# Time mixing moved from the weights to the data, and clamps and rounding moved to GpSimd, in an RWKV block with a gated FFN

## The reference

```python
xn = layernorm(x)
shifted = pad(xn, one token in front)[:, :-1]
k = (xn * mk + shifted * (1 - mk)) @ Wk          # v and r likewise, r through a sigmoid
# wkv: for each channel a recurrence over the 512 tokens, with a running maximum mx,
#   max_st = max(mx + td, k); num = e1s * num + e2s * v; den = e1s * den + e2s
s = (r * wkv) @ Wo
h = relu(xn @ w1[0] + b1[0])                     # expert 0 of the FFN alone has a weight
y = xn + h @ w2[0] + b2[0]
g = silu((y - mean(y)) * rsqrt(var(y) + 1e-5) * gamma + beta)
out = x + s * g
```

## Time and profile before

| | us |
|---|---|
| median of 3 runs | 128.43 (127.83 to 128.73) |
| the profiled execution | 127.27 |
| its span, first to last instruction | 125.4 |
| mean granted TensorE clock of it | 0.986 of full speed |

### The profile page before, as it was taken

How to read it: one execution, slowest core, us unless ns; L and a number is a source line. 1 busy time by engine, 2 the same in 40 slices (tenths; PEclk the granted TensorE clock), 3 DMA queues, 4 the chain that set the end, 5 groups by cost and what they waited for, 6 DMA issues and landing times.

```text
span 125.4 us, 1838 instructions
## 1 busy us (share of the span) xinstructions
PE 113.8 (91%) x448; PEld 77.4 (62%) x448; DVE 97.5 (78%) x206; ACT 105.9 (84%) x163; POOL 57.4 (46%) x87
## 2 busy tenths in 40 slices
...
GB/s 108 320 342 152 3 0 0 5 0 3 3 0 0 0 0 0 5 84 3 0 0 0 0 84 0 3 89 0 0 0 0 84 0 61 23 3 84 10 73 84
DMA packets 9433, 5.09 MB, mean 41 GB/s; under 512 B 464, under 2 KB 9168, under 8 KB 9424
## 3 DMA queue, kind: packets, MB, share of 16 engines
...
...
## 4 chain that ended last, share of the span: by engine, by line
PE 54%; DVE 2%; ACT 2%; issue 2%; ACTq 1%
PE ps_z L596 14%; PE ps_s L570 4%; PE ps_up L525 4%; PE ps_up L529 4%; PE ps_up L526 4%; PE ps_s L605 3%; PE ps_v L525 2%; PE ps_v L529 2%; PE ps_v L526 2%; PE ps_r L529 2%; PE ps_r L526 2%; PE ps_r L525 2%; PE ps_k L526 1%; PE ps_k L529 1%; PE ps_k L525 1%
## 5 line engine op out<-in xcount | busy, mean ns | idle before, releaser
L596 PE MATMUL ps_z<-hid,w_c 128*128 128x512 f32 x64 | 29.7, 594 | 0.0
L395 ACT ACTIVATE hid<-ps_up,vec 128x512 f32<-128x512 f32 x32 | 21.2, 682 | 2.5 <-PE ps_up L529 2.4
L596 PEld LDWEIGHTS ps_z<-hid,w_c 128*128 128x128 f32 x64 | 11.7, 190 | 10.1 <-issue 8.0
L323 POOL TENSOR_TENSOR dv<-v_sb 128x512 f32<-128x512 f32 x8 | 8.3, 1037 | 21.0 <-ACT v_sb L442 21.0
L315 POOL TENSOR_TENSOR sq_lo<-sq,sq_hi 128x512 fp32r<-128x512 f32 x8 | 11.0, 1371 | 12.6 <-ACT sq L403 12.0
L307 POOL TENSOR_SCALAR xn<-x_sb,neg_mean,rstd 128x128 f32<-128x128 f32 x28 | 16.7, 607 | 0.0
L525 PE MATMUL ps_up<-xT_hi,w_hi 128*128 128x512 f32 x32 | 16.3, 511 | 0.2
L739 DVE TENSOR_TENSOR_SCAN den<-e_keep,e_new 128x512 f32<-128x512 f32 x8 | 10.1, 1268 | 5.1 <-ACT e_new L428 4.7
L529 PE MATMUL ps_up<-xT_lo,w_hi 128*128 128x512 f32 x32 | 12.7, 398 | 0.0
L526 PE MATMUL ps_up<-xT_hi,w_lo 128*128 128x512 f32 x32 | 12.7, 397 | 0.0
L344 ACT ACT_TABLE_LOAD x8 | 10.3, 1283 | 2.4 <-issue 2.2
...
## 6 DMA issues: line engine op xcount, KB each, us to landing
...
vec<-vectors ACTq DMA_DIRECT2D x1, 6.0 KB, 3.2
```

Of the source, the lines that this page charges most:

```text
L395: act.activation(hid[b % 2][:, f, :], ps_up[f % 2][:, :], ACT.Relu, bias=vec[:, B1_COLUMN + f:B1_COLUMN + f + 1]).then_inc(done[f"hid{f}"], 1)
L596: ins = pe.matmul(ps_z[:, :], w2_c[:, f, :], hid[b % 2][:, f, :], start=False, stop=last)
```

## The change

- Token shift: the transposes now write into one of two banks `ps_z[b % 2]`, ACT copies it to an fp32 tile `xT` with one column of zeros in front (step `xT`), POOL makes `before_k`, `before_v`, `before_r` = shifted xT * (1 - m) (`Bk`, `Bv`, `Br`), DVE makes `mixed_k` and so on = `ps_z` * m + before (`ink`, `inv`, `inr`), and each projection is one fp32 matmul with the unchanged weights. The parts `w_now` and `w_before` are gone.
- `cx` is gone: the transposes leave their accumulation group open, and `z0` to `z3` add onto them.
- `xT_hi` is rounded from `xT` by POOL (by ACT for sequence 0), `w1_lo`, `gap_min` and `gap_max` are POOL's too, the last two with a second operation that changes nothing.
- One square, `sq` in fp32, and one fp32 matmul for `var`, now into the bank `ps_s`, which `s` and `back` share. `sq_hi` and `sq_lo` are gone.
- `th_r` writes back into `ps_r`, and `gated` reads it there.
- For sequence 7 the steps from `sq` to `res` and the store (`HALVED`) are issued in two halves of 256 tokens, in banks of their own.
- All four orders are new.

The diff, cut to its core:

```diff
     "pe": """
+        T:0 b2m up0:0 up3:0 k:0 up2:0 up1:0 z3:0 z2:0 z0:0 T:1 z1:0 v:0 up1:1 var:0 up0:1 k:1 up3:1 r:0
+        up2:1 T:2 z1:1 z0:1 z3:1 z2:1 up0:2 up1:2 var:1 v:1 up3:2 up2:2 k:2 T:3 r:1 z3:2 z1:2 z2:2 z0:2 k:3
+        up0:3 up1:3 var:2 up3:3 up2:3 s:0 v:2 z0:3 T:4 z1:3 z2:3 z3:3 back:0 up0:4 var:3 up1:4 r:2 k:4 s:1
+        up2:4 v:3 T:5 z0:4 up3:4 z2:4 r:3 z3:4 z1:4 k:5 var:4 up0:5 up1:5 v:4 back:1 up2:5 T:6 up3:5 s:2
...
     "act": """
+        ln_exp ve0 rs0 w1_hi neg_td xT:0 xT_hi:0 hid0:0 wo hid3:0 hid2:0 hid1:0 xT:1 e_keep:0 e_new:0 sq:0
+        v_sb:0 hid1:1 ln_den:0 ln_var:0 hid0:1 rstd2:0 silu_set th_g:0 th_a:0 xT:2 hid3:1 hid2:1 th_r:0
+        ln_exp e_keep:1 sq:1 hid0:2 e_new:1 hid1:2 ln_var:1 v_sb:1 rstd2:1 ln_den:1 hid2:2 hid3:2 xT:3
+        silu_set th_r:1 th_g:1 silu:0 th_a:1 sq:2 ln_exp e_keep:2 hid1:3 hid0:3 e_new:2 ln_var:2 hid3:3
...
     "dve": """
+        bnA:0 bnB:0 aggr1:0 norm1:0 bn:1 aggr1:1 one_minus cols xT_lo:0 w2_sum ink:0 bn:2 inr:0 aggr1:2
+        inv:0 mx:0 gap:0 bn:3 bn:4 aggr1:3 bn:5 xT_lo:1 den:0 ink:1 rel:0 inr:1 mx:1 zn:0 inv:1 aggr1:4
+        gap:1 dev:0 xT_lo:2 adev:0 ink:2 wkv:0 gated:0 inr:2 den:1 zn:1 rel:1 inv:2 mx:2 ink:3 gap:2 xT_lo:3
+        bn:6 inr:3 dev:1 aggr1:5 mx:3 gap:3 adev:1 wkv:1 inv:3 den:2 zn:2 bn:7 rel:2 aggr1:6 prod:0 den:3
+        xT_lo:4 res:0 ink:4 gated:1 dev:2 inv:4 adev:2 wkv:2 zn:3 inr:4 mx:4 rel:3 prod:1 gated:2 ink:5
...
     "pool": """
+        w1_lo neg_mean1:1 Bk:0 Br:0 Bv:0 w2_c rstd1:1 norm1:1 gap_min:0 gap_max:0 xT_hi:1 neg_mean1:2 Bk:1
+        Br:1 rstd1:2 Bv:1 norm1:2 dv:0 keep:0 xT_hi:2 Br:2 Bk:2 gap_max:1 neg_mean1:3 gap_min:1 rstd1:3 Bv:2
+        norm1:3 dv:1 neg_mean1:4 Bk:3 Br:3 xT_hi:3 keep:1 rstd1:4 gap_max:2 gap_min:2 neg_mean1:5 Bv:3
+        gap_max:3 gap_min:3 norm1:4 dv:2 neg_mean1:6 Bk:4 xT_hi:4 rstd1:5 keep:2 Br:4 Bv:4 norm1:5 rstd1:6
...
-        ps_x = bank("ps_x", T)
         ps_k = bank("ps_k", T)
         ps_v = bank("ps_v", T)
         ps_r = bank("ps_r", T)
         ps_up = [bank(f"ps_up{i}", T) for i in range(2)]
-        ps_z = bank("ps_z", T)
+        ps_z = [bank(f"ps_z{i}", T) for i in range(2)]
         ps_s = bank("ps_s", T)
-        ps_rows = ps_s[:, :].rearrange("p (j c) -> p j c", c=P)
+
+
+        def ps_var(half):
+            return {"": ps_s, "a": ps_up[0], "b": ps_up[1]}[half]
+
+        def ps_out(half):
+            return {"": ps_s, "a": ps_s, "b": ps_r}[half]
+
+        def ps_rows(half):
+            return {"": ps_s, "a": ps_k, "b": ps_v}[half][:, :].rearrange("p (j c) -> p j c", c=P)
...
+            def w1_low():
+                pool.wait_ge(prep["w1_hi"], 1)
+                pool.tensor_tensor(w1_parts[1][:, :], w1_in[:, :], w1_parts[0][:, :].bitcast(FP32),
+                                   ALU.subtract).then_inc(prep["w1_lo"], 1)
+
+            def high_part(b):
+                n = b % 2
+                after(pool, "xT", b)
+                for step in [f"up{f}" for f in range(NF)] + ["xT_lo"]:
+                    after(pool, step, b - 2)
+                pool.tensor_copy(xT_hi[n][:, :], xT[n][:, 1:]).then_inc(done["xT_hi"], 1)
+
+            def share_before(name):
+                which = "kvr".index(name)
+
+                def step(b):
+                    n = b % 2
+                    once(pool, b, "edges", EDGES)
+                    once(pool, b, "one_minus", 1)
+                    after(pool, "xT", b)
+                    after(pool, "in" + name, b - 2)
+                    pool.tensor_scalar(before[name][n][:, :], xT[n][:, 0:T], one_minus[:, which:which + 1], 0.0,
+                                       ALU.mult, ALU.add).then_inc(done["B" + name], 1)
+                return step
+
+            def lower(b):
+                n = b % 2
+                once(pool, b, "cols", 4)
+                after(pool, "gap", b)
+                after(pool, "e_new", b - 2)
+                pool.tensor_scalar(gap_min[n][:, :], gap[n][:, :], td[:, :], LOWEST, ALU.min,
+                                   ALU.max).then_inc(done["gap_min"], 1)
+
+            def upper(b):
+                n = b % 2
+                once(pool, b, "cols", 4)
+                after(pool, "gap", b)
+                after(pool, "e_keep", b - 2)
+                pool.tensor_scalar(gap_max[n][:, :], gap[n][:, :], td[:, :], HIGHEST, ALU.max,
+                                   ALU.min).then_inc(done["gap_max"], 1)
...
+                for step in ("Bk", "Bv", "Br", "xT_hi"):
                     after(act, step, b - 2)
-                act.activation(xT_hi[n][:, 1:], ps_x[:, :], ACT.Copy).then_inc(done["xT_hi"], 1)
+                act.activation(xT[n][:, 1:], ps_z[n][:, :], ACT.Copy).then_inc(done["xT"], 1)
...
+                act.activation(sq[b % 2][:, c], ps_z[b % 2][:, c], ACT.Square, bias=cb2[:, :]).then_inc(done["sq"], 1)
...
+                act.activation(ps_r[:, :], ps_r[:, :], ACT.Tanh, scale=0.5).then_inc(done["th_r"], 1)
...
             def transposes(b):
-                bank_x_free("T", b)
+                after(pe, "zn", b - 2)
                 if b > 0:
                     after_rows(pe, b)
                 for j in range(NT):
                     if b == 0:
                         pe.wait_ge(done["norm1"], j + 1)
-                    ins = pe.transpose(ps_x[:, j * P:(j + 1) * P], xn[b % 2][:, j, :], ident[:, :])
+
+                    ins = pe.matmul(ps_z[b % 2][:, j * P:(j + 1) * P], xn[b % 2][:, j, :], ident[:, :], start=j == 0,
+                                    stop=False, is_transpose=True, skip_group_check=True)
                 ins.then_inc(done["T"], 1)
...
+            def projection(name, dst, held):
                 which = "kvr".index(name)
-                now, before = ([part[:, :] for part in parts[which]] for parts in (w_now, w_before))
 
                 def step(b):
-                    n = b % 2
-                    once(pe, b, "w_hi_" + name, 2)
-                    once(pe, b, "w_lo_" + name, 2)
-                    once(pe, b, "edges", EDGES)
-                    after(pe, "xT_hi", b)
+                    if b == 0:
+                        pe.wait_ge(got["squares"], 16)
+                    after(pe, "in" + name, b)
                     for reader in held:
                         after(pe, reader, b - 1)
-                    high_passes(dst[:, :], now, xT_hi[n], 1, True)
-                    high_passes(dst[:, :], before, xT_hi[n], 0, False)
-                    after(pe, "xT_lo", b)
-                    low_pass(dst[:, :], now, xT_lo[n], 1, False)
-                    low_pass(dst[:, :], before, xT_lo[n], 0, True).then_inc(done[name], 1)
+                    pe.matmul(dst[:, :], w_in[:, which, :], mixed[name][b % 2][:, :], start=True,
+                              stop=True).then_inc(done[name], 1)
                 return step
...
+            def variance(b, half=""):
+                c = cut(half)
+                once(pe, b, "consts", 3)
+                after(pe, "sq", b, half)
+                if half:
+
+                    for f in range("ab".index(half), NF, 2):
+                        after(pe, f"hid{f}", b)
+                else:
+                    bank_s_free("var", b)
+                pe.matmul(ps_var(half)[:, c], averager[:, :], sq[b % 2][:, c], start=True, stop=True).then_inc(done["var"], 1)
...
+                    order = [name for name, _, i in tokens("pe") if name in CHUNKS and i == b]
+                    if order[0] == f"z{f}":
+
+                        for reader in ("xT", "xT_hi", "xT_lo", "ink", "inv", "inr"):
+                            after(pe, reader, b)
                     after(pe, f"hid{f}", b)
-                    last = [name for name, i in tokens("pe") if name in CHUNKS and i == b][-1] == f"z{f}"
-                    ins = pe.matmul(ps_z[:, :], w2_c[:, f, :], hid[b % 2][:, f, :], start=False, stop=last)
+                    last = order[-1] == f"z{f}"
+                    ins = pe.matmul(ps_z[b % 2][:, :], w2_c[:, f, :], hid[b % 2][:, f, :], start=False, stop=last,
+                                    skip_group_check=True)
...
+            def mix(name):
+                which = "kvr".index(name)
+
+                def step(b):
+                    n = b % 2
+                    after(dve, "T", b)
+                    after(dve, "B" + name, b)
+                    after(dve, name, b - 2)
+                    if b == 0:
+                        after(dve, "xT_hi", b)
+                    dve.scalar_tensor_tensor(mixed[name][n][:, :], ps_z[n][:, :], vec[:, which:which + 1],
+                                             before[name][n][:, :], ALU.mult, ALU.add).then_inc(done["in" + name], 1)
+                return step
...
+                dve.scalar_tensor_tensor(gated[n][:, :], ps_r[:, :], 1.0, wkv[n][:, :],
                                          ALU.add, ALU.mult).then_inc(done["gated"], 1)
```

(10 more changed lines are left out.)

318 lines of the change are left out of this document (125 added, 193 removed).

## The result

| | before | changed |
|---|---|---|
| median, us | 128.58 (4 runs) | 134.39 (133.66 to 134.84, 4 runs) |
| profiled execution, us | 127.27 | 134.19 |
| its span, us | 125.4 | 132.4 |
| mean granted clock | 0.986 | 0.955 |

The changed kernel is slower: ratio 1.046, 95% interval 1.041 to 1.050. The forecast was 124.0 us with a range of 119 to 131.5.

What follows compares the result with a forecast made beforehand. PE was taken to bound the middle before, DVE after: DVE busy 105.2 us plus 15.8 idle gave a 121.0 us span, 122.9 us profiled, scaled to a 124.0 us median; range 119 to 131.5, the forecast's own 121.5 to 127.

Steps and rivals of the forecast that it cites:

- five at 0.70: POOL, per sequence: Bk, Bv, Br, gap_min and gap_max at 0.70 us each, 3.5 us together.
- 9.1 us, some 74 us with the preparation: POOL's work per sequence and over the run, said to hide under DVE's 13.0 us per sequence.
- Rival (a): POOL and the lock it shares with DVE become the bound; slower, 136 us median at p = 1.2; chance 0.15.
- p = 0.92: Price in us of each of POOL's five new steps from which the lock's 8.4 + 5p per sequence decides.
- DVE's sum: DVE's busy time, additions less removals from 97.5, plus 1.0 for collisions with POOL: 105.2 us.
- the 4 us: DVE's total loss to collisions with POOL, up from about 3 us; bounds 2 and 10.
- its saving: PE passes removed less fp32 matmuls added: net -1.73 us per sequence, -13.8 for eight; busy time falling by some 12.
- The tail: From z:7 to the span's end, 12.2 us before: about -1.1 us through sq_lo's removal and the halves.
- the halves at 0.3: Last sequence's split steps: cost 0.4 us on ACT, save 0.7 us from silu on.
- The idle time in the middle: DVE's idle time in the middle, set equal to the gaps PE had before the change: 3.8 us.
- Rival (b): No change: longer path through four engines and fixed orders leave DVE idle 8 to 10 us mid-run, 128 to 130 us; chance 0.24.
- Rival (d): PE drops to its lower clock in a gap, a 0.235 us pass taking 0.47; chance 0.03 of a visible loss.

Runs made afterwards that it cites:

- e7: Changed kernel plus a tail of eleven POOL tensor_scalar forms, three times each: max then min medians 1987 and 1988 ns, min then max 687 ns; no kernel time given.
- e1: Changed kernel with gap_max on POOL as min then max instead of max then min: 126.03 us, ratio to before 0.979.
- e13: Kernel with cheap gap_max and xT_hi on ACT, the last sequence's steps from sq to res whole instead of in halves: 126.09 us, ratio to before 0.981.
- e8: Changed kernel with gap_max in the cheap form and xT_hi of all sequences rounded by ACT instead of POOL: 122.19 us, ratio to before 0.953.
- e5: Changed kernel with gap_max in the cheap form and 16 instead of 4 unused matmuls behind the first transposes: 125.48 us, ratio to before 0.977.

## Why the prediction was wrong, step by step

- **The failing step** is in the part on POOL: "an instruction with one column and one immediate takes 0.68 to 0.70 at 512 columns", and with it "five at 0.70". Four of the five did (0.69). gap_max took 2.00. I priced the instruction by its operands, and all rows that I had read were of pairs, mult with add and add with mult, that e7 shows to be cheap. My own far end of 1.78 for an unseen form was lower than what came. The prediction counted neg_mean among the forms with two immediates; it is a single mult, and at four columns it shows nothing of the price for 512. What the runs showed in place of the 0.70: 2.00 us for gap_max, worth 8.4 us of time (e1).
- **A second step that failed, a size**: "9.1 us, some 74 us with the preparation", which "fits under DVE's 13.0, and hides". With all five in the cheap form (e1) POOL is busy 84.9 us, 11 more. I priced its steps at their medians and put what the two engines lose to each other on DVE alone. In e1 the means are 0.93, 1.09 and 0.81 for before_k, before_r and before_v, 0.89 and 0.83 for the clamps, 1.21 for dv (median 1.04) and 0.58 for xn (median 0.44). And the work does not lie evenly: from 20 to 40 us POOL is busy 19.2 of 20 us even in e1.
- **Rival (a) named the place**: "it decides from p = 0.92". The mean of the five prices was (4 x 0.69 + 2.00) / 5 = 0.95. It had the right engine and the right kind of error, a price on POOL, with 0.15 of the chance, and where POOL is busy over 19 of 20 us it is as good as full, as (a) said. By that sum the span would have been 8 x (8.4 + 5 x 0.95) - 4 + 22 = 123 us, and it was 132.4. Its sum lacks two things that the trace shows: POOL's means above its medians, and the queues behind a late step, as ACT's 2.61 us and PE's 2.47 at 33 us. How much of the 8.4 us comes from POOL's sum of work and how much from gap_max being late for e_keep was not separated: no run put the same 1.3 us on a POOL step that nothing waits for.
- **DVE's sum held**: 104.2 busy against 105.2; ink 0.741 for 0.75, gated 0.678. DVE's loss to collisions was smaller than the 4 us that I had added up to. The rows that say so:

```profile
L752 DVE TENSOR_TENSOR_SCAN den<-e_keep,e_new 128x512 f32<-128x512 f32 x8 | 10.5, 1312 | 2.4 <-ACT e_new L473 2.3
L767 DVE TENSOR_TENSOR_SCAN dev<-keep,dv 128x512 f32<-128x512 f32 x8 | 10.4, 1303 | 0.3 <-POOL keep L384 0.2
L728 DVE SCALAR_TENSOR_TENSOR mixed_k<-ps_z,vec,before_k 128x512 f32<-128x512 f32 x8 | 5.9, 741 | 5.0 <-issue 4.9
L791 DVE SCALAR_TENSOR_TENSOR gated<-ps_r,wkv 128x512 f32<-128x512 f32 x8 | 5.4, 678 | 0.1
```

  dev is 0.09 above its median of the earlier trace rows, den 0.08 above its own of before, rel and adev are 0.02 and 0.04 above their own medians: 0.23 us per sequence, 1.8 us in all. POOL's side of the same collisions is the second failed step above.
- **ACT held**: 99.8 for 99.2.
- **PE's busy time did not show its saving**: 108.0 for 113.8, not 12 less. Records of a matmul are longer here: the first fp32r pass of up has a mean of 651 ns against 511 before, and up to 1.42 us where the clock was low. So the busy share is not PE's work.
- **The tail held**: from sq.a at 121.25 to the span's end it is 11.1 us, from sq_hi of before at 113.4 it was 12.0: about -0.9 for the -1.1 forecast. But in e13, without them, the new tail takes 15.1 us (from 109.4 to 124.5), 3 us more than the old one, where the text had the halves at 0.3. The prediction priced the halves by their fixed parts and overlap and left out that var, moved into `ps_s`, holds up back, res and s (2.1 us in e13), which the halves' own banks undo. That the term came out right was luck.
- **The idle time in the middle**, "where I give DVE the gaps that PE has today", 3.8 us: between 20 and 110 us it is 16.7 in the changed kernel (90 - 73.3), 9.0 with the clamp mended, 6.0 with xT_hi on ACT too. Rival (b), a middle idle time of 8 to 10 us, may be in that: e8 takes a step of the path and 4.3 us of POOL work away and gains up to 3.8 us.
- **With the one form mended** the kernel measures 126.0 us, inside the forecast's own 121.5 to 127; with xT_hi moved as well, 122.2.
- **Rival (d)**: the lower clock did appear, 0.83 from 10 to 20 and from 30 to 40 us of the changed kernel, each time behind a gap of PE of over 2 us (2.30 and 2.47), and 0.87 from 120 to 130. At the start it cost nothing that e5 could show. What it cost behind the gap at 34 us was not tried.
